# Row sums of a softmax: inverted in rows of 32, spread by a DRAM read with repeats, and multiplied in on GpSimd

## The reference

```python
q = (layernorm(x) @ Wq)   # 32 heads of 16
k, v = ctx @ Wk, ctx @ Wv # 8 key/value heads, each shared by 4 query heads
scores = einsum('bhqd,bhkd->bhqk', q, k) * 16 ** -0.5
probs = softmax(scores, axis=-1)
out = einsum('bhqk,bhkd->bhqd', probs, v)
x = x + out.reshape(b, s, 512) @ Wo
```

## Time and profile before

| | us |
|---|---|
| median of three timed runs | 293.88 |
| range of the runs | 293.35 to 294.14 |
| span of the profiled execution | 292.5 |
| what a timed run has beside that span | 0.9 to 1.6 (median 1.4) |
| PE busy in the span | 284.9 (97%) |
| DVE busy | 234.3 (80%) |
| ACT busy | 167.4 (57%) |
| POOL busy | 146.6 (50%) |

### The profile page before, as it was taken

The page is one execution under the profiler, slowest core; times in us unless marked ns, Lnnn a source line. Parts: engine busy times, 40 slices in busy tenths (PEclk is TensorE's granted clock), DMA queues, the critical chain, the costliest instruction groups (busy, mean ns, idle before and its releaser), DMA issues.

```text
span 292.5 us, 6282 instructions
## 1 busy us (share of the span) xinstructions
PE 284.9 (97%) x2136; PEld 224.2 (77%) x2136; DVE 234.3 (80%) x358; ACT 167.4 (57%) x284; POOL 146.6 (50%) x194
## 2 busy tenths in 40 slices
PE   7999999999999999999999999999999998999996
PEld 2689676856784675788988998989977687888875
DVE  5589987779978966665778868899977999998752
ACT  5965868876488398834445454466444475343310
POOL 6594332061414048504304661696097879875742
PEclk9999999999999999999999999999999999999999
DMA  7987454757377542490332515225635321000222
GB/s 224 348 224 277 147 210 146 242 182 256 90 252 233 170 128 94 148 255 20 103 100 51 135 26 131 57 60 145 172 107 156 109 72 38 2 0 3 108 89 92
DMA packets 35784, 39.52 MB, mean 135 GB/s; under 512 B 3928, under 2 KB 21848, under 8 KB 35754
## 3 DMA queue, kind: packets, MB, share of 16 engines
q1 hardware_dynamic: 35754, 39.13, 43.9%
HBM read 20.48 MB, written 6.29 MB: 92 GB/s over the span
## 4 chain that ended last, share of the span: by engine, by line
PE 81%; DVE 7%; POOL 4%; issue 3%; ACT 2%; DMA 1%; POOLq 0%; DVEq 0%; ACTq 0%
PE ps L494 16%; PE ps L496 15%; PE ps L495 15%; PE ps L783 5%; PE ps L693 5%; PE ps L859 4%; PE ps L750 3%; PE ps L772 3%; PE ps L898 3%; PE ps L871 2%; PE ps L796 1%; PE ps L909 1%; DMA out<-XB 1%; PE ps L706 1%; DVE xn L1225 1%
## 5 line engine op out<-in xcount | busy, mean ns | idle before, releaser
L1464 POOL TENSOR_TENSOR slot_l<-stg,slot_h 128x512 fp32r<-128x512 f32 x19 | 25.3, 1343 | 41.9 <-ACT slot_h L967 41.9
L1260 DVE TENSOR_REDUCE mx<-ps 128x8 f32<-128x1024 f32 x32 | 38.1, 1214 | 2.5 <-PE ps L750 2.2
L494 PE MATMUL ps<-xT_h,slot_h 128*128 128x256 f32 x128 | 36.9, 288 | 0.0
L496 PE MATMUL ps<-xT_h,slot_l 128*128 128x256 f32 x128 | 36.0, 281 | 0.0
L495 PE MATMUL ps<-xT_l,slot_h 128*128 128x256 f32 x128 | 35.9, 281 | 0.0
L1046 ACT ACTIVATE PT<-ps 128x1024 f32<-128x1024 f32 x32 | 31.2, 1026 | 4.2 <-PE ps L772 4.1
L1476 POOL TENSOR_SCALAR var_eps<-moments 128x1 f32<-128x1 f32 x32 | 7.5, 235 | 41.8 <-DVE moments L1221 40.9
L1506 POOL TENSOR_TENSOR zpart<-P 128x512 f32<-128x512 f32 x16 | 21.2, 1323 | 10.8 <-ACT P L1123 9.8
L1123 ACT ACTIVATE P<-ps 128x1024 f32<-128x1024 f32 x16 | 16.4, 1025 | 17.0 <-PE ps L871 17.0
L494 PEld LDWEIGHTS ps<-xT_h,slot_h 128*128 128x128 f32 x128 | 24.2, 189 | 1.7 <-issue 0.4
L992 ACT ACTIVATE xT_h<-ps 128x512 fp32r<-128x512 f32 x24 | 14.1, 600 | 18.3 <-PE ps L693 15.4
(11 more groups left out here) (175 smaller groups left out, 853.4 us busy)
## 6 DMA issues: line engine op xcount, KB each, us to landing
ctx_in<-in_ctx SPq DMA_DIRECT2D x20, 256.0 KB, 3.0
QS<-Q_h SPq DMA_DIRECT2D x16, 256.0 KB, 3.3
o_dram<-OTs SPq DMA_DIRECT2D x16, 256.0 KB, 2.2
Q<-Q1d SPq DMA_DIRECT2D x64, 64.0 KB, 2.1
X<-in_x SPq DMA_DIRECT2D x8, 256.0 KB, 5.4
stg<-in_wq SPq DMA_DIRECT2D x8, 256.0 KB, 5.1
QS<-Q_l SPq DMA_DIRECT2D x8, 256.0 KB, 3.2
O<-o_dram SPq DMA_DIRECT2D x8, 256.0 KB
```

Source lines behind the costliest of these rows:

```text
L494: eng.matmul(dst, left[0], right[0], start=start, stop=False)
L496: return eng.matmul(dst, left[1], right[0], start=False, stop=stop)
L1260: dve.tensor_reduce(mx[:, b % 2, :].rearrange("p (x r) -> p r x", r=REP)[:, r, :], wide(step).rearrange("p k (g t) -> p (k g) t", g=4), AX ...
L1464: pool.tensor_tensor(lo, src, hi.bitcast(F32), ALU.subtract).then_inc(w_lo_pool, 1)
```

## The change

Three things are changed in the first layer's attention, and all five lists are laid out anew.

- **The reciprocal.** ZR.b now writes the 4096 sums as 128 rows of 32 (z_in). DVE inverts them from SBUF (z_inv). The transpose on PE and its bank are gone.
- **The widening.** SP writes z_inv to DRAM (new step ZW.b, z_dram), and reads it back with each row of 512 repeated for 16 partitions (new step ZL.b, two transfers of 64 rows of 2 KB). This takes the place of ZE.b on ACT and of the four transposes of ZB.b on PE. ZL.b waits until ZW.b has landed, and until ZB of the sequence before has read z_wide.
- **The multiplication.** ZB.b stands on POOL instead of DVE, with both operands in SBUF.

```diff
                 elif kind == "ZR":
                     b = step[1]
                     consumed(sp, ("PV", b, 0))
                     consumed(sp, ("PV", b, 1))
-                    sp.wait_ge(zin_set, 1)
                     if b:
-                        filled(sp, ("ZT", b - 1))
-                    sp.dma_start(zin[0:KVH * REP, :], OTs[HD0:P:2 * HD0, :, :]).then_inc(z_loaded, 16)
+                        sp.wait_ge(z_inverted, b)
+                    sp.dma_start(z_in[:, :], OTs[HD0:P:2 * HD0, :, :]).then_inc(z_loaded, 16)
+                elif kind == "ZW":
+                    b = step[1]
+                    sp.wait_ge(z_inverted, b + 1)
+                    sp.dma_start(z_dram[b], z_inv[:, :]).then_inc(z_stored, 16)
+                elif kind == "ZL":
+                    b = step[1]
+                    sp.wait_ge(z_stored, 16 * (b + 1))
+                    if b:
+                        sp.wait_ge(o_scaled, b)
+                    for gq in range(2):
+                        sp.dma_start(z_wide[gq * HALF:(gq + 1) * HALF, :],
+                                     z_dram[b][:, gq, :].unsqueeze(1).broadcast_to([4, HD0, D])).then_inc(wide_loaded, 16)
...
-                elif kind == "ZT":
-                    pe.transpose(dst[:, 0:P], zin[:, :], ident[:, :]).then_inc(psum_full, 1)
-                elif kind == "ZB":
-                    for r in range(REP):
-                        last = pe.transpose(dst[:, r * P:(r + 1) * P], z_wide[:, r, :, :].rearrange("p g d -> p (g d)"),
-                                            ident[:, :])
...
-                elif kind == "ZE":
-                    act.activation(z_wide[:, :, :, :], rec[:, :, :].unsqueeze(3).broadcast_to([P, REP, KVH, HD0]),
-                                   ACT.Copy).then_inc(wide_ready, 1)
...
                 elif kind == "ZT":
                     b = step[1]
-                    filled(dve, step)
+                    dve.wait_ge(z_loaded, 16 * (b + 1))
...
-                    dve.reciprocal(rec[:, :, :].rearrange("p r (x j) -> p r x j", x=2),
+                        dve.wait_ge(z_stored, 16 * b)
+                    dve.reciprocal(z_inv[:, :], z_in[:, :]).then_inc(z_inverted, 1)
-                elif kind == "ZB":
-                    dve.tensor_tensor(O[:, :], O[:, :], place(step), ALU.mult).then_inc(dve_freed, 1)
...
+                elif kind == "ZB":
+                    b = step[1]
+                    pool.wait_ge(u_loaded, 16 * (b + 1))
+                    pool.wait_ge(wide_loaded, 32 * (b + 1))
+                    pool.tensor_tensor(O[:, :], O[:, :], z_wide[:, :], ALU.mult).then_inc(o_scaled, 1)
```

More of the change, by code:

```diff
@@ L47 @@
[L47 to L50, removed]
+LX.0 LX.1 LI LC.0.0 LW.wq0.1 LW.wkv.1 LW.wq0.0 LW.wkv.0 LC.0.1 LW.wq0.2 LW.wq0.3 LX.4 LX.2 LX.7 LC.0.2 LX.5 LO LX.3
@@ L56 @@
[L56 to L60, removed]
@@ L120 @@
-NM.4 L.wbase.2 L.wbase.0 LNs.3.6 XB.6 LNs.3.7 NM.1 NM.3 LNs.3.4 XB.7 LNs.3.2 LNs.3.5 LNs.3.3 XB.4 XB.5 LNs.3.1
-LNs.3.0 XB.2 XB.3 XB.0 XB.1
+SET.0 SET.1 SET.2 LNs.0.0 LNs.0.1 L.wkv.1 L.wq0.0 L.wq0.2 L.wq0.3 KM.0 LNs.0.2 LNs.0.3 CL.0.3 LNs.0.4 KM.1 KM.2
+LNs.0.5 KM.3 LNs.0.6 L.wo.0 L.wo.2 LNs.0.7 ZB.0 L.wo.1 KM.4 ZB.1 CL.0.6 CL.0.7 KM.5 L.w0.2 LNs.1.1 ZB.2 KM.6 LNs.1.0
+L.w0.0 KM.7 ZB.3 LNs.1.2 L.w0.1 ZB.4 CL.1.1 LNs.1.3 CL.1.0 ZB.5 L.wk1.0 LNs.2.0 L.wk1.1 LNs.2.1 LNs.1.5 ZB.6 LNs.1.4
+L.wk1.2 ZB.7 SET.5 LNs.2.3 L.wq1.1 L.wq1.0 SET.4 LNs.2.2 LNs.1.6 LNs.2.5 LNs.1.7 ZP.0 ZP.1 ZP.2 ZP.3 LNs.2.4 LNs.2.7
@@ L151 @@
 DVE_FREES = {s: n for n, s in enumerate(
[L152 removed]
+    s for s in DVE_ORDER if s[0] in ("XT", "K0", "Q0", "MX", "WO", "F0", "OX1", "LT", "K1", "Q1", "V1", "F1", "FH", "WE"))}
 HALVES = numbered(ACT_ORDER, "CT", "K0", "XT", "Q0", "OX", "LT", "K1", "Q1")
@@ L308, in build @@
         o_dram = nc.dram_tensor("o_dram", (B, KVH, 2 * HD0, D), F32, kind="Internal").ap()
+        z_dram = nc.dram_tensor("z_dram", (B, 4, 2, D), F32, kind="Internal").ap()
         ps = always.enter_context(nc.psum_tensor("ps", [P, 8, D], F32))
@@ L784, in _ @@
                                          PT[:, 2 * gq + j // 2, (j % 2) * D:(j % 2 + 1) * D], start=True, stop=True)
-                    last.then_inc(psum_full, 1)
-                elif kind == "ZT":
-                    b = step[1]
-                    dst = take(pe, step)
-                    pe.wait_ge(z_loaded, 16 * (b + 1))
-                    pe.transpose(dst[:, 0:P], zin[:, :], ident[:, :]).then_inc(psum_full, 1)
-                elif kind == "ZB":
-                    b = step[1]
-                    dst = take(pe, step)
-                    pe.wait_ge(wide_ready, b + 1)
-                    for r in range(REP):
-                        last = pe.transpose(dst[:, r * P:(r + 1) * P], z_wide[:, r, :, :].rearrange("p g d -> p (g d)"),
-                                            ident[:, :])
                     last.then_inc(psum_full, 1)
```

147 lines of the change are left out of this document (70 added, 77 removed).

## The result

Four timed runs of the changed kernel took 327.10, 330.52, 333.22 and 335.32 us, beside a median of 293.85 us for the kernel before on the same chip. Some executions fall into a slower state, so from here on a time is the median of the fast ones alone unless the text says otherwise: for the changed kernel two of the four, **328.8 us**, a loss of 35.0. The ratio is 1.1195, with a 95% interval of 1.1132 to 1.1258.

The account below looks back on a forecast made before the run. PE was taken as the bound, busy 284.9 of 292.5 us. The sum was 292.5 + 1.4 - 4.5 (PE spared) + 1.1 (start) + 7.0 (chain towards WO) = 297.5 us, slower; range 290.6 to 301.5, 8 times in 10.

Parts of the forecast that it names:

- What PE is spared: PE without the transposes of ZB and ZT, eight times each: -4.5 us, ends -4.4 and -5.6.
- The start: V0.0 on PE starts later because wkv.0 lands at 9.5 us behind other loads: +1.1 us, ends 0 and 1.6.
- ZL is the unknown: ZL's pair of reads, first issue to last landing: taken as 4.8 us, bounds 2.6 and 6.4.
- The upper bound of 6.4: ZL's two reads run one behind the other, 6.4 us for the pair: 303.5 us in all, chance 0.07.
- the rule that I had weighed: DMA splits over the largest engine count up to 16 dividing both slowest dimensions; both ZL reads share four: 303.5 us.
- The new chain towards WO: Three transfers in a row, then POOL, make PE wait ahead of WO: +7.0 us, 0.5 to 13 by ZL's time.
- the rival at 303.5: The two ZL reads run one behind the other, 6.4 us, giving 303.5 us; chance 0.07.
- GpSimd's multiplication, 1.3 us: Eight multiplications of 128x512 on POOL, 1.3 us each, costing nothing as throughput but counted in the chain towards WO.
- the rival that it holds DVE up: POOL's multiplications cost DVE up to 0.8 us each, 3 us more in all: 300.5 us; chance 0.04.
- Sequences 0 and 2 have room: WO.0 and WO.2 stand far enough behind for the new chain, so waits of only 0 to 0.5 us.

Follow-up runs that it names:

- f1: Changed kernel with ZL as one read of 16 repeats, OR in 16 blocks of 8 rows and ZR in two transfers: 309.3 us (1.0529).
- j1: f1 with the first part of all five lists as in the kernel before, and DM.2 ahead of ZL.0: 302.7 us (1.0291).
- k1: j1 with ZW and ZL left out of every sequence, z_wide filled once early, so outputs are wrongly scaled: 296.8 us (1.0113).
- i0: Kernel before with two repeated reads added for each sequence, into a DRAM tensor that nothing reads: 303.0 us (1.0303).
- e3: Changed kernel with one step moved in SP's list, DM.2 ahead of ZL.0 instead of two places behind it: 332.9 us (1.1328).
- g1: Changed kernel with only the multiplication ZB put back on VectorE instead of GpSimd: 325.6 us (1.1060).
- k2: j1 with the multiplication on VectorE, right ahead of OX: 306.6 us (1.0455).
- j2: j1 without the moved DM.2; ZR, reciprocal and ZW gone, ZL reads raw sums, ACT inverts them by logarithm and exponential: 328.1 us (1.1164).

## Why the prediction was wrong, by its own steps

The forecast had the way right: the time rose, with waits at the places named. The size was far off. These are the 35.0 us, as the runs take them off one after the other. In another order the parts would differ.

| what is taken away | from, to | us |
|---|---|---|
| few-engine form of ZL and OR (f1 also has ZR in two transfers) | 328.8 to 309.3 (f1) | 19.5 |
| new order of the start, ZL.0 ahead of DM.2 | 309.3 to 302.7 (j1) | 6.6 |
| ZW and ZL themselves, sixteen blocks | 302.7 to 296.8 (k1) | 5.9 |
| rest of the chain and of the new order, less what PE is spared | 296.8 to 293.9 (before) | 2.9 |

- **"What PE is spared", -4.5: right.** The steps of ZT and ZB are 5.3 us of the trace before, each counted from the end of the step ahead of it to its own end. That is within the ends of 4.4 and 5.6.
- **"The start", +1.1: mis-sized.** V0.0 came at 9.59 as worked out. The sentence that failed is that the steps up to 30 us stand in nearly the same order, "so I see nothing that takes this back": nothing gave it back, and something was added. I had read the order of PE and SP and not that of ACT, where W.wo.1 stands ahead of Q0.0.1 and waits 4.41 us for its chunk. ST.0.1 is 6.0 us late in the profile. j1, with the old start, has it where it was (31.44, before 31.66).
- **"ZL is the unknown", 4.8: mis-sized**, 6.7 in the mean. The upper bound of 6.4 (the two reads one behind the other) is what happened, and it had a chance of 0.07. The trace held more than I used: the 9 landing marks of each OR and the 5 of each ZR would have backed the rule that I had weighed, by which 4 blocks go over fewer engines.
- **"The new chain towards WO", +7.0, and the rival at 303.5: the step that failed.** Even with ZL at 6.4, the sum gave 13 us of stalls, and PE's idle time grew by 28.8. At the places that it named there were 11.3: WO.1 0.4 (1.9 forecast), WO.3 1.9 (1.0), ST.6.3 4.1 (1.5), WO.7 4.2 (1.0), WO.2 0.8 (0 to 0.5). The other 17.5 us stood elsewhere, 7.55 of them ahead of ST.2.3 and 1.8 ahead of ST.3.0, both waiting for DM. The sum counted each ZL only on its own chain to its own WO. What the runs showed in its place is that such a read delays what SP issues behind it: DM, ZR, the context. i0 shows it without any chain, 9.7 us beside 1.1 for the plain form. In e3, with DM.2 ahead of ZL.0, the 7.55 us gap is 1.32, and 4.1 us of the difference are by the move; yet the time did not fall. (A slip in the working: the chain of sequence 7 adds up to 8.02 us, not 8.05.)
- **Not in the sum at all: the clock.** PE's busy time was to fall by about 5 us and rose by 7.3, since the remaining steps are 12.7 us longer. k1 has 2.5 of that at a clock of 1.00 throughout, which leaves some 10 us. The estimate from the stretches at 0.50, half of 19.7 us, gives the same. I priced an idle microsecond of PE at one microsecond. That this part comes from the gaps is read from where it stands, and no run moved the clock alone.
- **GpSimd's multiplication, 1.3 us, and the rival that it holds DVE up:** 1.27 us measured. Its place costs something (g1 -3.2) or gains something (k2 +3.9), but it was not the cause. As for DVE, OT_l takes 881 ns in the mean in the changed kernel and 902 ns before: it is not held up more.
- **"Sequences 0 and 2 have room", 0 to 0.5: about right by its words.** PE is not idle ahead of WO.0, and for 0.8 us ahead of WO.2. But WO.0 is 16.5 us late, 10.5 of it gathered since ST.0.1, most of that in the gap ahead of ST.2.3, which no sequence of the sum had.

What stays open is the last 2.9 us, with the 5.3 of PE's relief inside it: about 8 us that ZR, OR, GpSimd in the chain and the new order cost between them. k1 keeps SP's waits, and does not part these. None of the 18 kernels that were run came under the kernel before.

## What to carry to other kernels

Before a transfer is priced by its bytes, look at the outermost dimension of both its sides: put 16 blocks there, the repeat itself if there is one. A slow transfer is priced by what is issued behind it on the same queue, not by its own reader alone; a cheap test is to add it, unread, to the kernel before. When a gap on PE is forecast, add that the steps behind it may run at the lower clock, and when lists are laid out anew, read the order of every engine at the start, not only of those that the change is about.

## What the runs showed of the hardware that was not expected

- A read of 4 blocks, each repeated 16 times, took 3.4 to 3.8 us for 128 KB with little ahead of it. A single read of 256 KB with the repeat outermost (16 blocks) took 3.4 us at best. Repeating a row is not slow in itself.
- 2 MB of added reads whose data nobody uses cost 9.7 us in one form (5 landing marks a transfer) and 1.1 us in the other (16 marks).
- Changing between logarithm and exponential on ACT loaded a table each time, 16 x 1283 ns in j2. The Trainium skill ("ScalarE: Activation LUTs", section "What ACT_TABLE_LOAD costs") gives the same 1283 ns for one load; the run agrees.
